# One slot instead of two for a head's f2 row in all partitions, with new outer step orders, in a two-layer graph network kernel

## What is computed

```python
h = maximum(layernorm(x), 0)
# layer 0: graph attention with 4 heads, then one output head ("BACK" in the kernel)
Wh = einsum('bnf,hfo->bhno', h, W_heads)
f1 = einsum('bhno,ho->bhn', Wh, a[:, :O]);  f2 = einsum('bhno,ho->bhn', Wh, a[:, O:])
e  = leaky_relu(f1[:, :, :, None] + f2[:, :, None, :], 0.01);  e = where(adj > 0, e, -1e9)
h  = elu(softmax(e) @ Wh)              # [B, 4, N, 256], heads side by side: 1024 features
out = elu(gat_heads(h, adj, W_out, a_out))          # the same with one head
y  = maximum(out @ w1 + b1, 0) @ w2 + b2 + out      # the ffn
x  = x + layernorm(y) * gamma + beta
# layer 1: graph convolution
h  = maximum(layernorm(x), 0)
x  = x + deg * (h @ Wi.T + b) + adj @ (h @ Wj.T)
```

## Time and profile before

| | us |
|---|---|
| median of three runs | 1366.93 (1364.19 to 1367.91) |
| the profiled execution, its own time | 1367.08 |
| span in its trace | 1365.3 |
| PE busy | 1310.1 (96%) |
| ACT busy | 1114.7 (82%) |
| DVE busy | 1106.9 (81%) |
| POOL busy | 374.9 (27%) |

### The profile page before, as it was taken

How to read it: one execution, slowest core, us unless ns; L and a number is a source line. 1 busy time by engine, 2 the same in 40 slices (tenths; PEclk the granted TensorE clock), 3 DMA queues, 4 the chain that set the end, 5 groups by cost and what they waited for, 6 DMA issues and landing times.

```text
span 1365.3 us, 27728 instructions
## 1 busy us (share of the span) xinstructions
PE 1310.1 (96%) x10109; PEld 1259.0 (92%) x10109; DVE 1106.9 (81%) x2848; ACT 1114.7 (82%) x2152; POOL 374.9 (27%) x252
## 2 busy tenths in 40 slices
...
DMA packets 42206, 53.32 MB, mean 39 GB/s; under 512 B 2836, under 2 KB 30808, under 8 KB 42072
## 3 DMA queue, kind: packets, MB, share of 16 engines
q1 hardware_dynamic: 42072, 51.56, 12.3%
...
## 4 chain that ended last, share of the span: by engine, by line
PE 80%; DVE 9%; ACT 6%; issue 3%; POOL 1%; DMA 0%; SPq 0%; ACTq 0%; DVEq 0%
PE ps L1101 59%; PE ps L1214 9%; PE ps L1316 4%; PE ps L1280 3%; DVE arg L986 2%; ACT arg L785 1%; DVE arg L1012 1%; PE ps L1253 1%; PE ps L1176 1%; DVE st L939 1%; ACT elu L806 1%; PE ps L1290 1%; ACT prob_hi L791 1%; DVE prob_lo L957 1%; ACT arg L781 1%
## 5 line engine op out<-in xcount | busy, mean ns | idle before, releaser
L658 POOL TENSOR_TENSOR hx_lo<-elu,hx_hi 128x512 fp32r<-128x512 f32 x128 | 168.8, 1321 | 694.0 <-ACT hx_hi L815 692.9
L1101 PE MATMUL ps<-prob_hi,whx_hi 128*128 128x256 f32 x1024 | 296.4, 289 | 3.8 <-DVE prob_lo L957 3.1
L1101 PE MATMUL ps<-prob_hi,whx_lo 128*128 128x256 f32 x1024 | 290.0, 283 | 0.0
L1101 PE MATMUL ps<-prob_lo,whx_hi 128*128 128x256 f32 x1024 | 289.9, 283 | 0.0
L785 ACT ACTIVATE arg<-arg,nmax 128x512 f32<-128x512 f32 x320 | 227.0, 713 | 3.0 <-DVE nmax L997 2.8
L781 ACT ACTIVATE arg<-arg,fcol 128x512 f32<-128x512 f32 x320 | 212.4, 714 | 12.9 <-DVE gmax L986 12.8
L957 DVE TENSOR_TENSOR prob_lo<-ps,prob_hi 128x1024 fp32r<-128x1024 f32 x160 | 195.2, 1220 | 31.1 <-ACT prob_hi L791 30.5
L986 DVE CUSTOM_DVE_ANT_0 arg<-f2bc,mask 128x512 f32<-128x512 f32 x308 | 217.3, 744 | 3.6 <-PE ps L1214 2.0
L1101 PEld LDWEIGHTS ps<-prob_hi,whx_hi 128*128 128x128 f32 x1024 | 196.2, 192 | 7.2 <-DVE prob_lo L957 4.2
L1101 PEld LDWEIGHTS ps<-prob_hi,whx_lo 128*128 128x128 f32 x1024 | 196.5, 192 | 0.3
L1101 PEld LDWEIGHTS ps<-prob_lo,whx_hi 128*128 128x128 f32 x1024 | 196.3, 192 | 0.0
...
## 6 DMA issues: line engine op xcount, KB each, us to landing
...
f_rows<-f2row SPq DMA_DIRECT2D x77, 2.0 KB
...
```

The costliest lines, as they stand in the source:

```text
L658: pool.tensor_tensor(out=hx[1][:, 2 * c.h:2 * c.h + 2, c.u * HN:(c.u + 1) * HN], in0=elu[:, c.buf, :, :], in1=hx[0][:, 2 * c.h:2 * c.h + 2 ...
L1101: i = pe.matmul(out, a, b_, start=(k == 0), stop=(k == n - 1))
```

## The change

- `F2S` goes from 2 to 1, so each f2bcast waits for the rowmax steps of the head just before it, and `f2bc` has one slot.
- w1 lands in slot 0 (`w1_st`), and the wait for `s_w1` moves from the f2bcast with d = 1 to the one with d = 0, the first.
- The lists FIRST and LAST of all five engines are written in another order. They hold the same words as before. ROUND is unchanged, word for word.

```diff
 FIRST = {
     "PE": """
...
-    turn_p:0@1 mix2:0@0 adj_turn:1@0 turn_p:1@1 mix2:1@0 attend:0@1 mix2:2@0 mix2:3@0 m1:31@1 turn_in@2 f2turn:-1@0 attend:1@1
-    turn_p:2@1 f2turn:2@1 m1:00@2 m1:01@2 f2turn:3@1 turn_p:3@1 attend:2@1 turn_p:4@0 f2turn:0@2 attend:3@1 m1:10@2 turn_p:5@0
...
+    adj_turn:1@0 mix2:0@0 mix2:1@0 turn_p:0@1 m1:30@1 mix2:2@0 mix2:3@0 m1:31@1 turn_p:1@1 f2turn:-1@0 turn_in@2 attend:0@1
+    f2turn:2@1 attend:1@1 turn_p:2@1 m1:00@2 turn_p:3@1 m1:01@2 attend:2@1 f2turn:3@1 turn_p:4@0 attend:3@1 m1:10@2 turn_p:5@0
...
@@ -266,7 +266,7 @@
-    F2S = 2
+    F2S = 1
@@ -341,7 +341,7 @@
-        w1_st = f2bc[:, 1, :].rearrange("p (k o) -> p k o", k=KC)
+        w1_st = f2bc[:, 0, :].rearrange("p (k o) -> p k o", k=KC)
@@ -610,7 +610,7 @@
                 if d >= F2S:
                     sp.wait_ge(max_made, 4 * (by_dma[d - F2S] + 1))
                 sp.wait_ge(f2_out[d % 4], 16 * (d // 4 + 1))
-                if d == 1:
+                if d == 0:
                     sp.wait_ge(s_w1, 1)
                 sp.dma_start(f2bc[:, d % F2S, :], f2_rows[d % 4].partition_broadcast(P)).then_inc(f2_spread[d % F2S], 16)
```

More of the change, by code:

```diff
@@ L22 @@
[L22 to L25, removed]
@@ L28 @@
+    f2turn:-1@2 m1:31@3 turn_in@4 attend:1@3
     """,
     "ACT": """
[L30 to L38, removed]
@@ L48 @@
[L48 to L56, removed]
+    norm_in@0 norm_in:1@0 norm_in_out@0 norm_in_out:1@0 wh_low:0@0 mask:0@0 mask:1@0 wh_low:1@0 wh_low:2@0 turn_in@0 wh_sum@0
@@ new lines @@
+    wh_low:3@0 turn_in:1@0 mask_end:0@0 mask_end:1@0 m1:00@0 gc_turn@0 m1:01@0 norm_in@1 m1:10@0 m1:11@0 rowmax:0@0
+    rowmath:0@0 rowmax:1@0 wo_prep:0@0 rowmath:1@0 wo_prep:1@0 norm_in_out@1 rinv:0@0 m1:20@0 scale:0@0 rowmax:2@0 m1:21@0
+    rowmath:2@0 rowmax:3@0 rinv:1@0 probs:0@0 scale:1@0 rowmath:3@0 m1:30@0 wo_prep:2@0 m1:31@0 wo_prep:3@0 rinv:2@0
+    wo_prep:4@0 elu_out:0@0 scale:2@0 probs:1@0 turn_in@1 wo_prep:5@0 rinv:3@0 w1_low@0 scale:3@0 probs:2@0 wo_prep:6@0
+    rowmax:6@0 rowmath:6@0 rowmax:7@0 elu_out:1@0 probs:3@0 rowmath:7@0 wo_prep:7@0 rinv:6@0 m1:00@1 elu_out:2@0 scale:6@0
@@ L101 @@
     "SP": """
[L102 to L109, removed]
+    f2send:2@-6 load@-4 f2bcast:2@-6 f2send:3@-6 f2bcast:3@-6 f2send:0@-5 f2bcast:0@-5 store@-8 f2send:1@-5 load_back@-7
@@ new lines @@
+    rowmath:6@-7 rinv:5@-8 scale:5@-8 probs:4@-8 conv_in:1@-9 rowmax:7@-7 rinv:6@-7 scale:6@-7 m1:10@-6 elu_out:3@-7
+    probs:5@-8 elu_out:4@-8 rowmath:7@-7 rowmax:8@-7 probs:6@-7 rowmax:9@-7 rinv:7@-7 rowmath:8@-7 elu_out:5@-8 norm_in@-5
+    scale:7@-7 rinv:8@-7 m1:11@-6 scale:8@-7 norm_in_out@-5 turn_out@-8 conv@-9 rowmath:9@-7 rowmax:0@-6 elu_out:6@-7
+    probs:7@-7 probs:8@-7 rowmax:1@-6 rinv:9@-7 rowmath:0@-6 rowmath:1@-6 scale:9@-7 elu_out:7@-7 elu_out:8@-7 probs:9@-7
+    rinv:0@-6 m1:20@-6 ffn2@-8 m1:21@-6 rowmax:2@-6 scale:0@-6 norm_ff@-8 rinv:1@-6 m1:30@-6 scale:1@-6 norm_ff_out@-8
@@ new lines @@
+    elu_out:9@-7 rowmath:2@-6 rowmax:3@-6 probs:0@-6 probs:1@-6 mix2:0@-7 x2@-8 rowmath:3@-6 norm_gc@-8 rinv:2@-6 mix2:1@-7
+    scale:2@-6 rinv:3@-6 elu_out:0@-6 scale:3@-6 m1:31@-6 norm_gc_out@-8 turn_in@-5 elu_out:1@-6 probs:2@-6 m1:00@-5
+    rowmax:4@-7 turn_gc@-8 m1:01@-5 rowmath:4@-7 probs:3@-6 rowmax:5@-7 rowmath:5@-7 rowmax:6@-6 rinv:4@-7 elu_out:2@-6
+    scale:4@-7 rowmath:6@-6 conv_in:0@-8 rinv:5@-7 scale:5@-7 rowmax:7@-6 conv_in:1@-8 probs:4@-7 elu_out:3@-6 rowmath:7@-6
+    m1:10@-5 rinv:6@-6 scale:6@-6 probs:5@-7 rowmax:8@-6 rowmath:8@-6 elu_out:4@-7 rinv:7@-6 probs:6@-6 rowmax:9@-6
@@ new lines @@
+    probs:2@-5 m1:00@-4 rowmax:4@-6 rowmath:4@-6 m1:01@-4 probs:3@-5 turn_gc@-7 rowmax:5@-6 rowmath:5@-6 rowmax:6@-5
+    elu_out:2@-5 norm_in@-3 rinv:4@-6 rowmath:6@-5 scale:4@-6 conv_in:0@-7 conv_in:1@-7 rinv:5@-6 scale:5@-6 norm_in_out@-3
+    elu_out:3@-5 probs:4@-6 rowmax:7@-5 m1:10@-4 probs:5@-6 m1:11@-4 rowmath:7@-5 rinv:6@-5 scale:6@-5 elu_out:4@-6
+    rowmax:8@-5 rowmath:8@-5 rinv:7@-5 rowmax:9@-5 elu_out:5@-6 probs:6@-5 scale:7@-5 conv@-7 turn_out@-6 rowmath:9@-5
+    rinv:8@-5 probs:7@-5 scale:8@-5 elu_out:6@-5 rowmax:0@-4 rowmath:0@-4 probs:8@-5 rinv:9@-5 elu_out:7@-5 scale:9@-5
@@ new lines @@
+    rowmax:1@-4 rowmath:1@-4 rinv:0@-4 scale:0@-4 rowmax:2@-4 m1:20@-4 rowmath:2@-4 rinv:1@-4 elu_out:8@-5 probs:9@-5 ffn2@-6
+    norm_ff@-6 probs:0@-4 norm_ff_out@-6 m1:21@-4 elu_out:9@-5 rowmax:3@-4 m1:30@-4 rinv:2@-4 scale:1@-4 x2@-6 rowmath:3@-4
+    norm_gc@-6 m1:31@-4 probs:1@-4 mix2:0@-5 norm_gc_out@-6 rinv:3@-4 mix2:1@-5 scale:2@-4 elu_out:0@-4 scale:3@-4 turn_in@-3
+    elu_out:1@-4 turn_gc@-6 probs:2@-4 m1:00@-3 rowmax:4@-5 m1:01@-3 rowmath:4@-5 rowmax:5@-5 probs:3@-4 rinv:4@-5
+    rowmath:5@-5 rowmax:6@-4 scale:4@-5 rinv:5@-5 rowmath:6@-4 conv_in:0@-6 elu_out:2@-4 rowmax:7@-4 scale:5@-5 conv_in:1@-6
@@ new lines @@
+    scale:2@-3 mix2:0@-4 x2@-5 norm_gc@-5 mix2:1@-4 rinv:3@-3 norm_gc_out@-5 m1:30@-3 probs:1@-3 elu_out:0@-3 scale:3@-3
+    m1:31@-3 turn_in@-2 elu_out:1@-3 probs:2@-3 turn_gc@-5 rowmax:4@-4 rowmath:4@-4 probs:3@-3 rowmax:5@-4 rowmath:5@-4
+    rinv:4@-4 m1:00@-2 scale:4@-4 norm_in@-1 m1:01@-2 rowmax:6@-3 elu_out:2@-3 probs:4@-4 conv_in:0@-5 rinv:5@-4 rowmath:6@-3
+    scale:5@-4 rowmax:7@-3 rowmath:7@-3 rowmax:8@-3 elu_out:3@-3 probs:5@-4 rinv:6@-3 elu_out:4@-4 conv_in:1@-5 scale:6@-3
+    elu_out:5@-4 rinv:7@-3 rowmath:8@-3 m1:10@-2 scale:7@-3 conv@-5 rowmax:9@-3 probs:6@-3 rowmath:9@-3 turn_out@-4 rinv:8@-3
```

295 lines of the change are left out of this document (146 added, 149 removed).

## The result

The changed kernel takes 1382.72 us in the median of four runs (1380.66 to 1386.84), the one before 1366.52 in four (1364.19 to 1367.91). The ratio is 1.0133, 95% interval 1.0116 to 1.0150: 18 us slower (15.8 to 20.5), and the medians lie 16.2 apart. The forecast was 1374.5, 7.5 above before. Its direction was right, its size less than half, and 1382.72 lies beyond the forecast's own range of 1371 to 1381, though inside the wide one of 1363 to 1385.

The account below looks back on a forecast made before the run. PE was taken to bound the repeated rounds, busy 555.98 of 556.00 us. Losses of 17.2 us by the slot minus gains of 9.7 by the orders gave +7.5, so 1374.5 us; range 1363 to 1385, the forecast's own 1371 to 1381.

Parts of the forecast that it names:

- the reordering may take half: Middle of LAST: the new order takes half of PE's 4.7 us idle time, -2.5 us, bounds 0 and -4.7.
- place 1: Where LAST begins: rowmax:6 stalls 3.2 us near 760.5, the steps queued behind it make attend:3 late by 3.0 us.
- rounds: Eight repeated rounds: cover 2.83 us at rowmax:6, about 0.3 us of each stall reaches PE, 2.4 us in all.
- place 2: One batch after LAST begins: four DVE steps again stand behind rowmax:6, costing PE 3.1 us.
- place 3: Two batches after LAST begins: one more step stands ahead of the old head's last maximum, costing 2.0 us.
- place at step @14: Last of the LAST places with steps queued behind the waiting rowmax: 1.7 us lost.
- the others in LAST: Five further LAST heads with cover under 3.3 us: 8.9 us of stalls, 3.7 reaching PE, DVE's idle time swallowing the rest.
- clock: One fall of PE's granted clock to 1.2 GHz behind a new stall: +1.3 us, bounds 0 and 5.
- rival C: Much slower: every stall reaches PE and the clock falls at each long one, 1388 us; chance 0.10.
- A: Faster: stalls fall into DVE's idle time at all but two places, 1361 us; chance 0.18 together with D.
- B: No change: losses of 10 to 12 us and gains of 9 to 10 cancel, 1367 to 1370 us; chance 0.22.
- D: The slot is never waited for, needing covers above 3.3 us everywhere; gains alone give 1357 us; chance 0.18 with A.

Follow-up runs that it names:

- e1: The changed kernel with the slot set back: new FIRST and LAST, two slots, w1 in slot 1; 1362.63 us, ratio 0.9982 to the kernel before.
- e2: New orders, two slots, w1 in slot 1 as in e1, but each f2bcast waits for the head just before it; 1383.79 us, ratio 1.0143.
- e3: New FIRST with the old LAST, two slots; 1362.57 us, ratio 0.9980 to the kernel before.
- e5: e1 with the old order in the last batch's tail alone, on PE, ACT, DVE and POOL; 1363.71 us, ratio 0.9987 to the kernel before.
- e7: The changed kernel with the f2bcast filling only 64 of 128 partitions, half the bytes; 1378.22 us, ratio 1.0099 to the kernel before.
- e10: e6 with the new order of LAST on SP alone, the other engines keeping the old one; 1378.89 us, ratio 1.0097 to the kernel before.
- e6: New FIRST and old LAST on all engines, with one slot; 1391.58 us, ratio 1.0192 to the kernel before.
- e11: New orders, two slots, with steps in DVE's LAST moved ahead of waiting rowmax steps; 1371.39 us, ratio 1.0044 to the kernel before.

## Why the prediction was right and wrong, step by step

**What failed.** Two terms of the sum were mis-sized. The gains of the new orders, 9.7 us, measure 2.2 (e1), and the losses by the slot, 17.2 us, measure 20.1 to 21.2 (e1 to the changed kernel and to e2). The first is 7.5 us of the miss and the second 3 to 4; the whole miss is 9 us by the medians and 10.5 by the ratio. The step behind the first is "the reordering may take half" and its like, shares of idle time without a wait that goes; the step behind the second is that DVE's idle time would swallow more than half of the five smaller stalls.

**The mechanism held.** SP issues 0.02 us behind the maximum, the landing takes 3.0 to 3.2, and rowmax:6 waits 3.09 us at place 1, for which 3.2 was forecast. DVE's waits on f2bc in LAST add to 18.3 us at eight places, where I had 21 at nine, if full; the other 2.4 of the 20.7 are in the repeated rounds, 0.17 to 0.49 in each, where I had 0.3 to 0.5.

**The sizes of single places held, the sum over LAST did not.** I set the start of each head's rowmax in the changed kernel, and in e2, against that in e1, which has the same orders. The starts are from the three traces, in which the order of DVE's list tells which maximum is which head's. The steps by which that difference grows, in us:

| | forecast | changed kernel | e2 |
|---|---|---|---|
| rounds | 2.4 | 1.8 | 1.9 |
| place 1 | 3.0 | 3.0 | 4.3 |
| place 2 | 3.1 | 4.0 | 3.1 |
| place 3 | 2.0 | 1.8 | 1.8 |
| place at step @14 | 1.7 | 5.9 | 3.3 |
| the others in LAST | 3.7 | 8.1 | 7.4 |
| clock | 1.3 | in the rows above | in the rows above |
| sum | 17.2 | 24.6 | 21.8 |

These are single executions; by the medians the sum is 20.1 for the changed kernel and 21.2 for e2, against 17.2. The three places near the traced rounds are right within their clock. The term of 3.7 for "the five others", set at under half of their 8.9 us because DVE's idle time would take the rest, should have been near the whole, and the 1.7 at step @14 double. The idle time of 12.3 us in each round is real, but it swallows nothing here: DVE idles mostly while it waits for ACT, and those waits stay. From rowmax:4 of batch 8 to rowmax:8 of batch 15 DVE waits 72.3 us for ACT in e1's trace and 72.4 in the changed kernel's, while its waits for f2bc go from 0.4 to 18.3. Of 20.7 us more waiting on DVE in e2, 21.2 arrived at the end. That is the mechanism of rival C, "every stall reaches PE", which I gave 0.10; its time of 1388 was too high since it took 25 us of stalls and 5 of clock, 30 in all, where 20 to 21 came, clock included. That it comes as near as it does is in part luck, since its gains were 7.5 us too high as well.

**The clock.** Where e2 and the changed kernel differ at one place, the clock explains it. Stretches of the changed kernel behind its waits near 849, 973 and 1186:

```profile
850.20:853.60 3.40, 3.26 (x15) 3.29 (x16) 3.37 (x8) 2.74 (x7) 2.07 (x2) 0.50 0.02 5
973.10:976.50 3.40, 3.40 (x19) 3.40 (x17) 3.37 (x5) 1.96 (x3) 1.48 (x1) 0.50 0.36 127
1184.70:1191.50 6.80, 5.62 (x18) 4.76 (x19) 5.72 (x12) 4.71 (x9) 0.84 (x1) 0.50 0.00 0
```

And the same of e2, behind its wait near 766, and then at two of these places:

```profile
766.90:770.30 3.40, 3.13 (x14) 3.16 (x15) 3.33 (x9) 3.40 (x7) 0.00 (x0) 0.50 0.12 19
845.00:853.60 8.60, 6.48 (x41) 5.23 (x40) 6.61 (x19) 7.31 (x17) 1.01 (x1) 1.00 0.09 30
1180.00:1195.00 15.00, 11.92 (x90) 11.18 (x89) 13.73 (x33) 10.35 (x22) 1.26 (x1) 1.00 0.05 18
```

The same waits at the same places lowered the clock to 1.2 GHz in one execution and not in the other. With the fall, place 1 is 1.3 us longer in e2, place 2 0.9 in the changed kernel, place @14 2.6 with the longer fall, and near 973, among "the others", 1.4 in the changed kernel. So 1.3 for a fall was right, one fall was too few for the profiled execution (1386.84 us), and about right for the three others (1380.66 to 1382.83), whose mean granted clock is 0.989 instead of 0.983.

**The gains.** 9.7 us were forecast, e1 has 2.2 by the median (0.8 to 4.0).
- FIRST: -4.5 forecast. In e3's profile a head's rowmax starts 3.8 us earlier than in before, from batch 3 (near 236) to the end; by the medians FIRST is worth 2.3 (before's executions lie from 1362.5 to 1368.8 in that series, and the profiled one, 1367.08, is in their upper half). PE's wait of 2.53 at turn_p:4@0 is 1.57 in the changed kernel, not under 1, and the clock behind it is full, as forecast. From 30 to 199.9 PE idles 13.5 us in the changed kernel and 14.6 in before, 1.1 less in all. The row of turn_p:4@0 in PE's timeline of the changed kernel:

```profile
126.74 0.98 PE L1214 MATMUL ps<-ident,arg 128*128 128x128 f32 x7 [1.57 <-DVE arg L1012]
```

- Middle of LAST and 1239 to 1310: -2.5 and -2.0 forecast. e1 against e3, which is all of LAST with its tail, gives 0.0. "The reordering may take half" was no working from a row. PE idles 3.2 us from 914.4 to 1239 in e1 and 4.2 in before, so there was little to have, and none of it came out at the end.
- The tail: -0.7 forecast. With the old tail e5 is 1.1 us above e1 (0.7 by the ratios), so the new one gives about what was forecast, but within the noise.

**The rivals.** A fell: in the changed kernel and in e2 the stalls came out in full and none of them landed in DVE's idle time. B fell with it. D was excluded by the cover of 2.83, rightly: DVE waited in each round. C's mechanism was right. With a landing of 2.6 us, as I had worked it out by the rule of the Trainium skill, the rounds would have been free and the time 1369. 256 KB take 3.2 us here, and the rounds were not free.

The Trainium skill, "DMA: Bandwidth & Descriptors", section "Anatomy of one DMA — SWDGE (gpsimd) path", gives that rule for DMAs that GpSimd issues. These are issued by SP, which I had passed over, so the 3.2 us say nothing against the page. Its part that goes with the bytes, at 436 GB/s, makes an estimate of 0.3 us for 128 KB; this case has 0.4 (e7).

**What I didn't see.** The wait on SP holds up what is behind it, f2send and the load of x. With one slot, the new LAST of SP pays 12.7 us (e10 against e6). I had looked at this queue in the set-up only, and cost it at nothing; in the changed kernel that is right.

Not settled: why each move of e11 costs what it does. Head by head against e1, in one trace each, e11 loses 0.6 us at place 1, 2.2 near 930 (PE waits 1.46 at 927), 4.0 near 968 (the wait of 2.92, and a fall of the clock) and 1.6 near 1041 (PE waits 1.36). That is 8.4 of the 8.8 us; that the moved steps make these waits is argued from the order and not tested move by move.
